# Cross-attention on one core: ScalarE's order in the output phase rewritten, and reciprocals spread in two DMAs over 128 partitions instead of four over 64

## What is computed

```python
qh = (q @ Wq + bq).reshape(Bn, Tq, H, DK)
kh = (k @ Wk + bk).reshape(Bn, Tk, H, DK)
vh = (v @ Wv + bv).reshape(Bn, Tk, H, DK)
attn = jnp.einsum('bqhd,bkhd->hbqk', qh, kh) * mask[None]
attn = attn - jnp.max(attn)            # one maximum over everything
attn = jnp.exp(attn) * mask[None]
attn = attn / (jnp.sum(attn, axis=-1, keepdims=True) + 1e-15)
out = jnp.einsum('hbqk,bkhd->bqhd', attn, vh).reshape(Bn, Tq, H * DK)
x = out @ Wo + bo + residual
mu, var = mean(x), mean((x - mu) ** 2)
return (x - mu) / jnp.sqrt(var + 1e-05) * gamma + beta
```

## Time and profile before

| | us |
|---|---|
| median of 3 runs | 1738.48 |
| lowest, highest | 1737.42, 1738.65 |
| the profiled execution | 1738.39 |
| its span, first to last instruction | 1736.5 |
| scores phase, about | 0 to 905 |
| one unit of the output phase | 24.37 |

### The profile page before, as it was taken

How to read it: one execution, slowest core, us unless ns; L and a number is a source line. 1 busy time by engine, 2 the same in 40 slices (tenths; PEclk the granted TensorE clock), 3 DMA queues, 4 the chain that set the end, 5 groups by cost and what they waited for, 6 DMA issues and landing times. The chain is left out here.

```text
span 1736.5 us, 30465 instructions
## 1 busy us (share of the span) xinstructions
PE 1619.3 (93%) x10501; PEld 796.7 (46%) x10501; DVE 1151.8 (66%) x2138; ACT 935.5 (54%) x1383; POOL 544.1 (31%) x778
## 2 busy tenths in 40 slices
PE   4999999999999999999983999999999999999997
PEld 4445555455554555545531344444444444444443
DVE  6666555565556655566542777878778787878774
ACT  6755555555555555555534555555555555555542
POOL 0000000000000000000000567677666767677677
PEclk8999999999999999999995999999999999999999
DMA  6463444534445444453327999999999999999971
GB/s 231 146 226 121 164 176 151 222 122 160 172 157 217 127 154 172 163 211 128 153 97 247 265 308 314 290 286 292 313 318 295 291 313 316 278 293 297 310 234 73
DMA packets 92556, 382.11 MB, mean 220 GB/s; under 512 B 7520, under 2 KB 12768, under 8 KB 74592
## 3 DMA queue, kind: packets, MB, share of 16 engines
q1 hardware_dynamic: 92512, 381.53, 65.7%
HBM read 250.43 MB, written 131.07 MB: 220 GB/s over the span
## 5 line engine op out<-in xcount | busy, mean ns | idle before, releaser
L78 PE MATMUL ps_o<-u,p_hi 128*128 128x512 f16 x1024 | 389.7, 381 | 5.0 <-DVE p_lo L985 5.0
L69 PE MATMUL ps_s<-x_hi,g_hi 128*128 128x512 f16 x1024 | 389.1, 380 | 3.7 <-ACT s L496 3.7
L79 PE MATMUL ps_o<-u,p_hi 128*128 128x512 f16 x1024 | 389.4, 380 | 0.0
L80 PE MATMUL ps_o<-u,p_lo 128*128 128x512 f16 x1024 | 389.2, 380 | 0.0
L71 PE MATMUL ps_s<-x_hi,g_lo 128*128 128x512 f16 x1024 | 388.8, 380 | 0.0
L70 PE MATMUL ps_s<-x_lo,g_hi 128*128 128x512 f16 x1024 | 388.6, 380 | 0.0
L496 ACT ACTIVATE s<-ps_s,c_bias 128x512 f32<-128x512 f32 x256 | 176.1, 688 | 314.1 <-PE ps_s L71 311.0
L1052 POOL MEMSET zeros<- 128x256 f32 x1 | 0.3, 311 | 905.9 <-POOLq L138 905.9
L985 DVE TENSOR_TENSOR p_lo<-ps_p,p_hi 128x512 f16<-128x512 f32 x256 | 175.4, 685 | 126.3 <-ACT p_hi L902 126.0
L616 DVE TENSOR_TENSOR score_max<-score_max,tile_max 128x1 f32<-128x1 f32 x257 | 40.7, 158 | 310.5 <-ACT s L496 308.8
L912 ACT ACTIVATE y<-y,shift,rstd 128x512 f32<-128x512 f32 x128 | 104.1, 813 | 243.4 <-POOL shift L1073 238.9
(11 more groups left out here) (90 smaller groups left out, 2363.1 us busy)
## 6 DMA issues: line engine op xcount, KB each, us to landing
r_bc<-reciprocals SPq DMA_DIRECT2D x128, 512.0 KB, 8.1
scores<-s SPq DMA_DIRECT2D x30, 2048.0 KB, 7.6
x<-xT_in SPq DMA_DIRECT2D x32, 1024.0 KB, 9.5
u_halves<-u_out SPq DMA_DIRECT2D x64, 512.0 KB, 3.2
s_more<-scores SPq DMA_DIRECT2D x16, 2048.0 KB, 16.3
u<-u_halves SPq DMA_DIRECT2D x16, 2048.0 KB, 22.3
y<-x_in SPq DMA_DIRECT2D x32, 1024.0 KB, 18.1
out<-y SPq DMA_DIRECT2D x31, 1024.0 KB, 12.3
```

The costliest lines, as they stand in the source:

```text
L69: pe.matmul(out, lhs_hi, rhs_hi, start=first, stop=False)
L78: pe.matmul(out, lhs_hi, rhs_hi, start=False, stop=False, skip_group_check=True)
L79: pe.matmul(out, lhs_hi, rhs_lo, start=False, stop=False, skip_group_check=True)
L80: return pe.matmul(out, lhs_lo, rhs_hi, start=False, stop=False, skip_group_check=True)
```

## The change

ScalarE's function `group` gets a new order, in which `fill` of the fourth bank and the norms of tiles 2 and 3 move into the next unit's step. The first group is written out too, since it has no unit before. In `spread_r`, the two DMAs by head become one whose source has both heads. The counts that VectorE waits for are halved with the number of DMAs.

```diff
                 for k in range(2):
-                    for h in range(2):
-                        rows = r_d[u % UNITS, h:h + 1, 4 * k:4 * k + 4, :].rearrange("a p t -> a (p t)")
-                        sp.dma_start(r_bc[rows_of(h), u % 2, 4 * k:4 * k + 4, :].rearrange("r p t -> r (p t)"),
-                                     rows.to_broadcast([NK, 4 * TT])).then_inc(bc_in[u % 2][k], 16)
+                    rows = r_d[u % UNITS, :, 4 * k:4 * k + 4, :].rearrange("h p t -> h (p t)").unsqueeze(1)
+                    sp.dma_start(r_bc[:, u % 2, 4 * k:4 * k + 4, :].rearrange("r p t -> r (p t)"),
+                                 rows.to_broadcast([2, NK, 4 * TT])).then_inc(bc_in[u % 2][k], 16)
...
-            def group(g, last):
+            def group(g, first, last):
                 for u in range(UNITS):
...
-                    halves(0, 1)
+                    behind = lambda t: None if first and u == 0 else norm(g if u else g - 1, (u - 1) % UNITS, t)
                     if more3:
                         tiny(n + 3)
+                    halves(0)
+                    fill(n, 3)
+                    halves(1)
+                    if more3:
                         exps(n + 3, u + 3, 0)
-                    halves(2, 3)
+                    behind(2)
+                    halves(2)
+                    if more3:
+                        exps(n + 3, u + 3, 1)
+                    halves(3)
+                    behind(3)
                     if more:
                         fill(n + 1, 0)
+                    halves(4, 5)
                     norm(g, u, 0)
...
-            for t in range(TB):
+            for t in range(TB - 1):
                 fill(0, t)
...
-                    dve.wait_ge(bc_in[s][p // 4], 16 * n - 16 * s + 32)
+                    dve.wait_ge(bc_in[s][p // 4], 8 * n - 8 * s + 16)
```

More of the change, by code:

```diff
@@ L918, in group @@
                     halves = lambda *ps: [round_p(n + 1, s, p) for p in ps] if more else None
-                    halves(0, 1)
+                    behind = lambda t: None if first and u == 0 else norm(g if u else g - 1, (u - 1) % UNITS, t)
                     if more3:
                         tiny(n + 3)
+                    halves(0)
+                    fill(n, 3)
+                    halves(1)
+                    if more3:
                         exps(n + 3, u + 3, 0)
-                    halves(2, 3)
+                    behind(2)
[4 more added lines that the diff above has]
+                    behind(3)
                     if more:
                         fill(n + 1, 0)
+                    halves(4, 5)
                     norm(g, u, 0)
-                    if more3:
-                        exps(n + 3, u + 3, 1)
-                    halves(4, 5)
                     if more:
                         fill(n + 1, 1)
+                    halves(6, 7)
                     norm(g, u, 1)
-                    halves(6, 7)
                     if more:
                         fill(n + 1, 2)
[L936 to L939, removed]
+                if last:
+                    norm(g, UNITS - 1, 2)
+                    norm(g, UNITS - 1, 3)
             act.wait_ge(o_written, 1)
@@ L956, in _ @@
                 round_p(0, 0, p)
-            with act.Fori(0, NG - 1) as g:
-                group(g, False)
-            group(NG - 1, True)
+            group(0, True, False)
+            with act.Fori(1, NG - 1) as g:
+                group(g, False, False)
+            group(NG - 1, False, True)
         @block.vector
```

## The result

| | before | after |
|---|---|---|
| median of 4 runs, us | 1738.57 | 2848.57 |
| lowest, highest | 1737.42, 1739.21 | 2847.81, 2848.79 |
| span of the profiled execution | 1736.5 | 2846.2 |

The ratio is 1.6386, with a 95% interval of 1.636 to 1.6412. The changed kernel is 64% slower. The loss is mostly time in which the engines stand.

The account below looks back on a forecast made before the run. TensorE, closely followed by the DMA engines, bound the output phase; after the change SyncE's queue would, with two-engine spreads. Fourth spread at 1075, 28 periods of 57.0 less 4.9, landing and a 42 us tail gave 2751 us, range 2600 to 2900.

Parts of the forecast that it names:

- Two engines: Each merged spread in the output phase runs on two of sixteen DMA engines, one per head.
- The rival with sixteen engines: All sixteen DMA engines share the merged spread, 4.9 us per engine: 1695 up to 1738 us; chance 0.12.
- The one with a longer chain: Two engines, other work no longer hidden by the spread: 62 to 90 us per unit, 2900 to 3700 us; chance 0.03.
- the turn: In SyncE's queue a spread waits for its reciprocals' store while the DMA engines run dry: 2.1 us per unit.
- The rate: The merged spread moves 26.7 GB/s per engine, as loads do, one engine per half: 39.3 us per unit.
- The rival at the half rate: Two engines run the merged spread at 13.4 GB/s: period 92.7 us, time about 3907 us; chance 0.05.
- The period: One unit of the output phase takes 39.3 + 12.3 + 2.1 + 3.3 = 57.0 us, between 53.7 and 58.6.
- meetings: The two spreading engines meet score, x and u loads, which halves the rate: 3.3 us per unit, from 0 to 4.9.
- The start: Output phase's first spreads: the first issued at 939.0 us, the third at 1034, the fourth at about 1075.
- The end: Last spread issued at 2666 us, its second half landing at 2707, then 42 us to the end at 2749.
- Hidden behind the spread: The next reciprocals are ready 8 us into a 39.3 us spread; SyncE's queue sets the period, ScalarE's gain is worth nothing.
- ScalarE's order by itself: Earlier second-half exponentials take TensorE's 1.48 us wait out of 29 units: a gain between 0 and 43 us.

Follow-up runs that it names:

- the deals: Kernel before, its four spreads' 64 source copies written as 2 x 32, 4 x 16 or 8 x 8: 3070.02, 2435.08 and 2138.07 us.
- sixteen: Changed kernel with reciprocals stored in 16 rows by 8 stores, the merged spread reading 16 rows by 8 copies: 1806.09 us, ratio 1.0379 to before.
- spread_alone: Kernel before with only the two merged spreads, ScalarE's old order kept: 2842.13 us, ratio 1.6329.
- order_alone: Kernel before with only ScalarE's new order, the four old spreads kept: 1747.41 us, ratio 1.0043.
- thirtytwo: Changed kernel with 32 rows of reciprocals, sixteen stores, four copies from the sums' matmul, spread 32 by 4: 1754.23 us, ratio 1.0088 to before.
- late: Kernel before with each unit's spread issued one step later, behind the score load: 1742.88 us, ratio 1.0033.
- hybrid: thirtytwo with norm 3 ahead of the exponentials, norm 2 and the fourth fill back in their own unit: 1763.84 us, ratio 1.0139 to before.

## Why the prediction was right, and where 97 us are missing

*Two engines.* Right, and read from the right rows: the packets of the earlier trace rows gave two engines for the store, and the deals show that the same count decides for the spread. (The two-unit stretch has 260 small packets where the text's own count gives 240 + 16; over the whole runs the counts fit to the packet.) The signs that the text named are there: halves that land at 22 and 44 us, a share of 0.38 at 123 GB/s, TensorE at 43%. Only the spreads, 57.2 and 62.2 us apart in turn, go over the 54 to 59 named. The rival with sixteen engines (0.12) falls. The one with a longer chain (0.03) too: in the twenty units from 1503.38 to 2703.32, no packet is in flight for 34.0 us and one alone for 16.7, so each of the two engines stands 2.1 us per unit, which is the turn, and no more.

*The rate.* Right: 26 GB/s per engine while the spread runs alone, against 26.7 taken from loads. The rival at the half rate (0.05) falls for this kernel, but a half rate does occur, in sixteen and at times in the deals. The prediction's reason, which halves are written into, was the right kind of reason and too simple: sixteen writes into all 128 partitions and still runs at half.

*The period.* 59.8 us in place of 57.0, just above its bounds of 53.7 and 58.6. The packets of the same twenty units (60.0 us each) give the terms. The spread's 256 packets of 8 KB take 90.3 us of engine time per unit, 45.2 on each of the two engines; at the 309 ns of a packet that runs alone, 128 of them take 39.6. So 5.6 us are meetings with the loads. With the turn of 2.1 us, 12.7 are left for the two engines' part of the other transfers. Term by term: spread by itself 39.6 for 39.3; other transfers 12.7 for 12.3; turn 2.1 for 2.1; meetings 5.6 for 3.3. **The term that was mis-sized is the meetings**, above even the 4.9 us that the text gave as its upper bound and didn't take. The period is over its bound, and the time stays in its range because that left four more us per period for something missed. The last spread is issued 1674.3 us after the fourth, the text had 1591: 83 of the 97 us.

*The start.* The fourth spread was issued at 1085.90, the text had 1075. The third is right (1034.31 for 1034), but the loads before it weren't through:

```profile
1034.31 5.70 SPq L760 DMA_DIRECT2D r_bc<-reciprocals  x2
...
1085.90 1.06 SPq L760 DMA_DIRECT2D r_bc<-reciprocals  x2
```

Issuing it takes SyncE 5.70 us in place of some 1.06, and its first packet of 8 KB starts only at 1044.2, behind packets of the loads, so the fourth follows 51.6 us later, not 41. Another 11 us. With the 83 that makes 94, and the last spread indeed comes at 2760.17 for 2666.

*The end.* VectorE's first tiles of either half of the last unit, in its timeline:

```profile
2782.37 1.30 DVE L987 TENSOR_TENSOR ps_p<-s_more,r_bc 128x512 f32<-128x512 f32 x2 [21.38 <-DMA r_bc<-reciprocals]
...
2803.75 0.70 DVE L987 TENSOR_TENSOR ps_p<-s_more,r_bc 128x512 f32<-128x512 f32 x1 [14.44 <-DMA r_bc<-reciprocals]
```

The halves land 22.2 and 43.6 us after the issue at 2760.17, where the text had 40.8 for the second (about 3 us more), and from there to the end of the span are 42.5 us for 42. The 94 and these 3 are the 97.

*Hidden behind the spread.* Right for ScalarE's gain: between spread_alone and after the order moves 6 to 10 us, and to the worse, not 43. Right as well that the queue decides, and not an engine. In the timeline above, SyncE reaches the y store 7.6 us after the spread's issue, so the y store and score load are in the queue in time, and the loads' own landing is what ScalarE stands for (795 us).

*ScalarE's order by itself.* The range of 0 to 43 us didn't hold: 8 us lost. The step that failed is that the first exponentials' start was taken as fixed by ScalarE's program. In every second unit it is set by the score load, as soon as ScalarE asks earlier. The giving back through GpSimd is what the text warned of, a unit of 24.8 us if norms come late: order_alone has 24.65, with GpSimd at work or waiting for a norm for 24.0 of it. The text took that as the end of the gain, and it is a loss, since before has 24.4.

*What stays open.* Why sixteen and the deals run at half rate: which partitions the engines write at a given time, and which rows they read, the trace has no row for, and the mechanism is only argued. And what sets before's 24.4 us per unit to the last us: taking load off the DMA engines (thirtytwo), asking for exponentials earlier (order_alone) and taking the turn out of the queue (late) each gain nothing by themselves. Opening the loop through ScalarE, GpSimd, SyncE's queue and the score load (hybrid) doesn't gain either. That would fit several waits that are equally late, the exchange of tiles between ScalarE and GpSimd among them, but no run shortens all of them at once, and the cause stays open.

## What to carry to other kernels

Before two DMAs are merged, look at the outermost count of each operand, copies of stride 0 included: in these kernels the smaller of the two set the number of engines. The number of completion packets tells how many engines a DMA runs on, and can be counted in the profile of an existing kernel. A transfer that covers more partitions isn't faster if it runs on fewer engines, and with all sixteen it can still run at half rate, so measure its GB/s over 16 x share. Where a queue runs in one order, a step moved ahead of another on an engine can be given back by what now stands behind it (here norms, and through them GpSimd), so follow the loop once around before counting a removed wait as a gain.

## What the runs showed of the chip beyond that

- When two DMA engines have a long row of work, SyncE's issue instructions themselves take long: 9.86, 16.38 and 9.21 us for single transfers in the timeline of after, where thirtytwo issues the like in 0.36 to 0.94 (its timeline has 0.41 and 0.36 for a y store and a score load). SyncE then can't do anything else.
- Transfers that meet slow each other. In after 898 of 5120 spread packets take over 330 ns, where one alone takes 309, and the 16-KB packets of the loads have a mean of 823 ns for 620 in before.
- The cut of a spread's source, 16 rows by 8 copies or 32 by 4, changes the rate from 14.5 to 26.1 GB/s per engine at equal bytes, destination and number of engines.
- TensorE idles for over 30 us in each unit of after, and the granted clock has a mean of 0.70 in 1100 to 2700, with stretches at 0.5, the lower of its two levels (1.2 GHz of 2.4). Its busy time rises from 1619.3 to 1730.0 us for the same instructions. No run separates its cost; the two DMA engines stand only 2.1 us per unit, so there is little that TensorE could still hold up.
